# A graph network's count stage reordered: edge loads split by 96, 28 and one row, four count batches ahead of the products, half of the first weight sums on VectorE

## The reference

```python
# layer 0 (t5 norm, then RGCN with F = 286 columns and 2 relations)
out = x @ W_root + bias
for r in range(2):
    w = (edge_type == r)
    msg = h_src @ W_rel[r] * w[:, None]
    sums = segment_sum(msg, dst); cnt = segment_sum(w, dst)
    out = out + sums / maximum(cnt, 1.0)[:, None]
y = elu(out) @ wo_weight; h = x + y
# then x = layernorm(x + h)
# layer 1: the same with 8 relations of 1024 x 1024, a root product,
#          and a gate: z = [u, x] @ w_gate + b_gate; h = tanh(u) * z + x * (1 - z)
# then x = layernorm(x + h)
```

## Time and profile before

| | |
|---|---|
| median of 3 runs | 890.87 us (890.82 to 891.12) |
| the profiled execution | 891.17 us, of it the span 889.2 us |
| TensorE matmuls busy | 834.6 us (94%) |
| VectorE | 674.5 us (76%) |
| ScalarE | 447.7 us (50%) |
| POOL | 16.1 us (2%) |
| DMA moved | 63.42 MB, mean 71 GB/s |
| mean granted TensorE clock | 0.975 |

### The profile page before, as it was taken

One profiled execution on the slowest core, in us unless ns is written; L12 is line 12 of the kernel. 1 busy time (PEld: TensorE's weight loads), 2 busy tenths in 40 slices (PEclk: granted clock), 3 DMA queues, 4 the chain that ended last, 5 costly groups with the idle time before them and its releaser, 6 DMA issues.

```text
span 889.2 us, 16319 instructions
## 1 busy us (share of the span) xinstructions
PE 834.6 (94%) x6332; PEld 591.8 (67%) x6332; DVE 674.5 (76%) x975; ACT 447.7 (50%) x633; POOL 16.1 (2%) x38
## 2 busy tenths in 40 slices
PE   2569999899989999999999999999999999999996
PEld 1435574445876876876866867867868768769442
DVE  5985569689987778778778777677777787777877
ACT  3984555556465544445355356255354444445721
POOL 1000000000000000000000000000000000000000
PEclk9669999999999999999999999999999999999998
DMA  8100026120222021021120220220220210311302
GB/s 266 62 23 31 0 99 235 72 95 1 95 96 95 2 96 68 28 95 33 61 94 1 93 94 0 94 94 0 94 94 0 94 66 30 119 34 63 119 24 92
DMA packets 30734, 63.42 MB, mean 71 GB/s; under 512 B 1389, under 2 KB 5097, under 8 KB 30697
## 3 DMA queue, kind: packets, MB, share of 16 engines
q1 hardware_dynamic: 30181, 62.64, 19.9%
q10 hardware_dynamic: 516, 0.26, 0.1%
HBM read 57.71 MB, written 5.18 MB: 71 GB/s over the span
## 4 chain that ended last, share of the span: by engine, by line
PE 76%; DVE 16%; ACT 4%; issue 3%; DVEq 0%; POOL 0%; ACTq 0%; POOLq 0%
PE psP L1081 44%; PE psA L1151 19%; PE psP L928 5%; PE psA L917 3%; DVE wsplit L1326 2%; DVE wsplit L1320 2%; PE psP L1006 1%; DVE p_mem L1364 1%; PE psP L885 1%; DVE wsplit L1455 1%; PE psA L873 1%; DVE xT L1292 1%; DVE stats L1530 1%; DVE cu_mem L1574 1%; DVE p_mem L1363 1%
## 5 line engine op out<-in xcount | busy, mean ns | idle before, releaser
L1081 PE MATMUL psP<-wsplit,xT 128*128 128x256 f16 x2592 | 296.4, 273 | 3.2 <-ACT vec L767 2.8
L1081 PEld LDWEIGHTS psP<-wsplit,xT 128*128 128x128 f16 x2592 | 254.3, 98 | 37.5 <-issue 3.1
L1151 PE MATMUL psA<-p_mem,cu_mem 128*128 128x512 f16 x800 | 175.3, 379 | 0.0
L1081 PE MATMUL psP<-wsplit,x 128*128 128x256 f16 x1296 | 150.3, 273 | 1.7 <-DVE key_mem L1640 1.5
L1151 PEld LDWEIGHTS psA<-p_mem,cu_mem 128*128 (+1 forms) x800 | 78.2, 98 | 91.0
L1081 PEld LDWEIGHTS psP<-wsplit,x 128*128 128x128 f16 x1296 | 126.7, 98 | 16.8 <-issue 2.2
L1326 DVE SCALAR_TENSOR_TENSOR wsplit<-stage,sc,wsplit 128x1024 f16<-128x1024 f32 x90 | 114.8, 1279 | 27.2 <-ACT wsplit L611 27.2
L611 ACT ACTIVATE wsplit<-stage,sc 128x1024 f16<-128x1024 f32 x90 | 100.6, 1137 | 15.0 <-DVE sc L1228 9.1
L1605 DVE SCALAR_TENSOR_TENSOR cu_mem<-psA,coef,cu_mem 128x512 f32<-128x512 f32 x80 | 60.0, 750 | 32.9 <-PE psA L1151 30.9
L611 ACT ACTIVATE wsplit<-x,sc 128x1024 f16<-128x1024 f32 x54 | 61.7, 1143 | 39.2 <-PE psP L1081 32.5
L1326 DVE SCALAR_TENSOR_TENSOR wsplit<-x,sc,wsplit 128x1024 f16<-128x1024 f32 x54 | 69.2, 1282 | 10.3 <-ACT wsplit L611 10.2
(11 more groups left out here) (189 smaller groups left out, 800.8 us busy)
## 6 DMA issues: line engine op xcount, KB each, us to landing
stage<-in_L_gnn_weight SPq DMA_DIRECT2D x16, 2048.0 KB, 7.8
stage<-in_L_gnn_w_gate SPq DMA_DIRECT2D x4, 2048.0 KB, 7.8
x_home<-x SPq DMA_DIRECT2D x5, 512.0 KB, 2.6
x<-x_home SPq DMA_DIRECT2D x5, 512.0 KB, 5.6
stage<-in_L_gnn_W_rel SPq DMA_DIRECT2D x4, 572.0 KB, 11.1
x<-in_x SPq DMA_DIRECT2D x4, 512.0 KB, 9.6
xT<-in_L_gnn_root SPq DMA_DIRECT2D x1, 2048.0 KB, 8.0
stage<-in_L_gnn_root SPq DMA_DIRECT2D x1, 2048.0 KB, 7.8
```

Of the source, the lines that this page charges most:

```text
L1081: last = nc.tensor.matmul(psP[:, bank, (col + tt) * FB:(col + tt + 1) * FB], lhs[tt](a, c), split_block(n, b)[:, c, :], start=(first and t ...
L1151: last = nc.tensor.matmul(psA[:, (NT * h + t) % 2, :], cnt8[:, r, s, t * P:(t + 1) * P], p_part[h][a][:, s, :], start=(s == 0 and a == 0), ...
```

## The change

Three things are done together.

- `load_edges` takes three loads for each array: rows 0 to 95 with all 256 columns, rows 96 to 123 with all 256, and the last row's 160. There are twelve loads instead of eight, six on SP's queue and six on ACT's.
- `AHEAD` becomes 4. Tile 0 has three batches *behind* each of its four quarter products; tiles 1 to 4 have one batch ahead of each, as before.
- VectorE sums chunks 4 to 7 of the first weights with one reduction and two small steps; ScalarE sums 0 to 3.

With these, orders change. ScalarE squares four tiles before it spreads keys, spreads the two-type keys of all windows at once, and the eight-type keys of windows 40 to 319 after its sums. VectorE spreads the low bits of windows 40 to 319 after its sums. Table 6 stands between the low parts of chunks 3 and 4. The norm weights are transposed ahead of the x tiles, into a bank of `psP`. The order check's matmul stands after tile 0, the register loads ahead of the last tile.

```diff
-AHEAD = NB - 4 * NT
-FIRST = AHEAD + 2
+FIRST_PART = 3
+AHEAD = NB - 4 * (NT - 1) - 4 * FIRST_PART
...
+            def span(v, p0, p1):
+                return bass.AP(v.tensor, v.offset + p0 * RUN, [[RUN, p1 - p0], [1, SPAN]])
             for a, v in arrays:
-                engine.dma_start(edges[:, a, 0:RUN], v.rearrange("(p e) -> p e", e=RUN)).then_inc(loaded, 16)
+                engine.dma_start(edges[0:ROWS16, a, :], span(v, 0, ROWS16)).then_inc(loaded, 16)
             engine.wait_ge(edges_padded, 2)
             for a, v in arrays:
-                engine.dma_start(edges[0:EP - 1, a, RUN:SPAN],
-                                 v[RUN:EDGES].rearrange("(p e) -> p e", e=RUN)[:, 0:SPAN - RUN]).then_inc(loaded, 16)
+                engine.dma_start(edges[ROWS16:EP - 1, a, :], span(v, ROWS16, EP - 1)).then_inc(loaded, 16)
+                engine.dma_start(edges[EP - 1:EP, a, 0:RUN], v[EDGES - RUN:EDGES].unsqueeze(0)).then_inc(loaded, 16)
...
@@ ScalarE
-            square_x(0)
-            square_x(1)
-            spread_keys(0, EARLY)
-            square_x(2)
+            for t in range(4):
+                square_x(t)
+            spread_keys_8(0, EARLY)
+            spread_keys_2(0, NWIN)
             split_hi(0, 0, xT, X_GAIN)
-            spread_keys(EARLY, NWIN)
-            square_x(3)
+            square_x(4)
             split_hi(0, 1, xT, X_GAIN)
...
-            copy_batches(3, 4)
-            w0_sum(0)
-            copy_batches(4, 8)
-            w0_sum(1)
-            copy_batches(8, 10)
+            w0_sums_first()
+            copy_batches(3, AHEAD)
+            spread_keys_8(EARLY, NWIN)
             act.wait_ge(w0_scaled, 1)
             w0_high(0)
-            copy_batches(10, AHEAD)
             w0_high(1)
@@ TensorE
+            count_batches(3, AHEAD)
+            count_tile(0, count_first=False)
             pe.wait_ge(wrong_ready, 2)
+            pe.wait_ge(low_spread, 2)
             nc.tensor.matmul(psC[0:1, 0:RUN + KT], ones[0:EP, :], wrong, start=True, stop=True).then_inc(wrong_counted, 1)
-            count_batches(3, AHEAD)
+            with pe.Fori(1, NT - 1) as t:
+                count_tile(t)
             pe.wait_ge(flag_ready, 1)
             wrong_order = pe.value_load(flag[0:1, 0:1], min_val=0, max_val=EP)
-            count_tile(0)
-            with pe.Fori(1, NT) as t:
-                count_tile(t)
+            count_tile(NT - 1)
@@ VectorE
+            def w0_sums_second():
+                half = slice(DC // 2, DC)
+                dve.wait_ge(w0_loaded[1], 48)
+                step(nc.vector.tensor_reduce(am0[:, half], st0[:, half, :], AX.X, ALU.add, apply_absolute_value=True))
+                step(tt(am0[:, half], am0[:, half], lnwT[:, half], ALU.mult))
+                stt(am0[:, half], am0[:, half], -1.0, am0[:, half], ALU.mult, ALU.max).then_inc(w0_sums, 1)
...
             split_x_lo(4)
-            onehot_batches(5, 6)
...
+            dve.wait_ge(lnwT_ready, 1)
+            w0_sums_second()
+            spread_low(EARLY, NWIN, 2)
...
-            onehot_batches(AHEAD, FIRST - 1)
+            dve.wait_ge(keys8_spread, 2)
+            onehot_batches(AHEAD, AHEAD + 2)
...
             w0_low(0)
-            onehot_batches(FIRST - 1, FIRST)
+            onehot_batches(AHEAD + 2, AHEAD + 3)
             w0_low(1)
+            onehot_batches(AHEAD + 3, AHEAD + 2 * FIRST_PART)
...
             onehot_tile(0, first=True)
-            with dve.Fori(1, NT) as t:
+            onehot_batch(AHEAD + 4 * FIRST_PART, 0)
+            first_sums(0, 1)
+            dve.wait_ge(wrong_counted, 1)
+            nc.vector.tensor_reduce(flag[:, :], psC[0:1, 0:RUN + KT], AX.X, ALU.max).then_inc(flag_ready, 1)
+            for n in range(1, 4):
+                onehot_batch(AHEAD + 4 * FIRST_PART + n, n % 2)
+                if n == 2:
+                    first_sums(1, 0)
+            with dve.Fori(2, NT) as t:
                 onehot_tile(t)
```

More of the change, by code:

```diff
@@ L385, in scale_col, with block_batches @@
             return i if i <= U_WO else 2 + slot
-        def block_batch(t, n):
-            return 4 * t + (AHEAD + n)
+        def block_batches(t, n):
+            if isinstance(t, int) and t == 0:
+                return [(k, k % 2) for k in range(AHEAD + FIRST_PART * n, AHEAD + FIRST_PART * (n + 1))]
+            return [(4 * t + (NB - 4 * NT + n), n % 2)]
         def by_twos(engine, k0, k1, batch):
@@ L543, in square_x, with spread_keys_8, spread_keys_2 @@
                                      scale=1.0 / D).then_inc(rms_std_ready, 1)
-            def spread_keys(j0, j1):
+            def spread_keys_8(j0, j1):
+                act.wait_ge(keys_gathered, 1)
+                nc.scalar.activation(key_spread[:, j0:j1, 0:R1], psP[:, 4, j0:j1].unsqueeze(2).broadcast_to([P, j1 - j0, R1]),
+                                     ACT.Copy).then_inc(keys8_spread, 1)
+            def spread_keys_2(j0, j1):
                 act.wait_ge(keys_gathered, 2)
[L548 to L551, removed]
+                nc.scalar.activation(key_spread[:, j0:j1, R1:REL_ALL],
+                                     psP[:, 3, j0:j1].unsqueeze(2).broadcast_to([P, j1 - j0, R0]),
+                                     ACT.Copy).then_inc(keys2_spread, 1)
             def split_hi(k, t, dst, gain):
@@ L639, in _, with w0_sums_first @@
             st0, hi0, _ = unit_weights(U_W0)
-            def w0_sum(a):
+            def w0_sums_first():
                 act.wait_ge(lnwT_ready, 1)
[L644 to L648, removed]
+                act.wait_ge(w0_loaded[0], 48)
+                for c in range(DC // 2):
+                    nc.scalar.activation(w0_land[:, c, :], st0[:, c, :], ACT.Abs, scale=lnwT[:, c:c + 1],
                                          accum_out=am0[:, c:c + 1]).then_inc(w0_sums, 1)
@@ L692, in _ @@
             wo_sum()
+            act.wait_ge(flag_ready, 1)
+            wrong_order = act.value_load(flag[0:1, 0:1], min_val=0, max_val=EP)
             copy_tile(NT - 1)
@@ L934, in blocks_ready, with count_tile @@
                 pe.wait_ge(wlo_ready, n)
-            def count_tile(t):
+            def count_tile(t, count_first=True):
                 for n in range(4):
                     h, a = n // 2, n % 2
-                    count_batch(block_batch(t, n), n % 2)
+                    if count_first:
+                        for k, b in block_batches(t, n):
+                            count_batch(k, b)
                     if a == 0:
@@ L948, in count_tile @@
                         last.then_inc(q_full, 1)
+                    if not count_first:
+                        for k, b in block_batches(t, n):
+                            count_batch(k, b)
+            pe.wait_ge(lnw_loaded, 16)
+            nc.tensor.transpose(psP[:, 2, 0:DC], lnw[:, :], ident[0:DC, 0:DC]).then_inc(lnw_turned, 1)
             turn(0, 0, xs, xs_ready)
@@ L953, in _ @@
             turn(0, 2, xs, xs_ready)
+            pe.wait_ge(keys2_spread, 1)
+            pe.wait_ge(lnwT_ready, 1)
             count_batches(1, 2)
[L955 to L957 removed]
             turn(0, 3, xs, xs_ready)
@@ L1409, in _ @@
             spread_low(0, EARLY, 1)
+            dve.wait_ge(lnw_turned, 1)
+            nc.vector.tensor_copy(lnwT[:, :], psP[:, 2, 0:DC]).then_inc(lnwT_ready, 1)
             dve.wait_ge(consts_ready, 7)
-            dve.wait_ge(keys_spread, 2)
+            dve.wait_ge(keys8_spread, 1)
+            dve.wait_ge(keys2_spread, 1)
             onehot_batches(0, 1)
@@ L1464, in onehot_tile @@
                     if not (first and n < 2):
-                        onehot_batch(block_batch(t, n), n % 2)
+                        for k, b in block_batches(t, n):
+                            onehot_batch(k, b)
                     if n == 0 and not first:
```

33 lines of the change are left out of this document (13 added, 20 removed).

## The result

The changed kernel takes **892.91 us** (median of 17 runs, 891.76 to 894.47); the kernel before, run beside it, 891.47 us (17 runs, 890.64 to 892.92). The ratio is 1.0017, 95% interval 1.0009 to 1.0024: slower by 1.4 us. Forecast were 895.6 us, a change of +4.7. The sign is right, and the time lies in the range of 8 in 10, 890.0 to 898.5.

The account below looks back on a forecast made before the run. TensorE was taken as the bound from the second quarter product (62.66 us), VectorE close behind. Terms -9.4 + 4.6 + 9.5 = +4.7 on the median 890.87 gave 895.6 us; own range 893.5 to 897.2, 8 in 10 890.0 to 898.5.

Parts of the forecast that it names:

- the new wait: VectorE ahead of table 6, held by the count of batch 4 queued behind Q0: 4.5 us, 47.9 to 52.4.
- Edge loads: Kernel start: loads cut into 96, 28 and 1 rows bring the first table to 17.25 instead of 19.35.
- the rest of the span moves as a block: Behind the loop over tiles: nothing changes but a register load, so the rest shifts with the loop.
- What is queued there: VectorE and TensorE around Q0: table 6 waits 4.5 us; the second quarter product starts at 57.9, before 62.66.
- third rival: VectorE isn't held at table 6; Q4 at 67.8, total 888.1 us, 886.4 with POOL early; chance 0.09.
- Q4: Fifth of TensorE's 20 quarter products, numbered from 0; forecast to start at 75.35 against 70.59.
- Q0: First of TensorE's 20 quarter products; forecast to start at 47.9 instead of 57.29, 9.4 us sooner.
- Q1 at the low level: Second quarter product, run at TensorE's low clock after idling about 3.6 us: ends at 61.6, against 60.2 at high.
- The walk through tile 0: Quarter products with three batches behind each, tables waiting for counts: 17.45 us to Q4 instead of 7.93, +9.5.
- the register load: TensorE's load of the flag's register, now ahead of the last tile: taken at 0, covered by queued matmuls.
- Q5: Sixth of TensorE's 20 quarter products, the forecast's landmark: start at 78.4 against 73.67, +4.7 us.
- second rival: Smaller loss: POOL ready by 9.0 (-1.65), second quarter product at high clock (-1.9): +1.15, 892.0 us; chance 0.14.

Follow-up runs that it names:

- both ways of taking it away: Changed kernel with all eight low parts ahead of table 6: 886.66 us; or with TensorE counting batches 4 and 5 ahead of Q0: 885.60 us.
- the two counts moved forward: Changed kernel with TensorE counting batches 4 and 5 ahead of Q0 instead of behind it: 885.60 us, 0.9942 against the kernel before.
- the clock held up ahead of Q0: Changed kernel with 28 unread matmuls of 429 columns on TensorE until Q0: 891.48 us, 1.0014 against the kernel before.
- the delayed kernel: Kernel before with 20 unread matmuls on TensorE ahead of the degree matmuls: 894.58 us, 1.0036.
- the sums back on ScalarE: Changed kernel with all eight sums on ScalarE and no reduction on VectorE: 896.51 us, 1.0059 against the kernel before.

## Why the prediction was right and wrong

**The step that failed.** The new wait was there as forecast; terms of the sum were mis-sized. Forecast were +4.7 us, measured +1.4, so 3.3 are missing. The largest error is in step "Edge loads", which took 2.1 us off the start because it held POOL's identity at 10.62: by themselves these loads took 4.2 us off the kernel, and the identity was ready at 9.53 there and by 9.0 in the changed kernel. That is 2.1 of the 3.3. The rest of the change was put at 6.8 (4.7 + 2.1) and cost 5.6 us, 1.2 less. By the profiles it moved the degrees by 6.65 us (mean 119.63 against 112.98 with the edge loads alone), so up to there it was priced nearly right. What is missing lies mostly behind them, in a term that was put at nothing, "the rest of the span moves as a block": the rest was 1.0 us shorter than before in the mean of three profiles, by falls of the clock. Why they were fewer stays open. The single steps follow.

**Right: the new wait.** Step "What is queued there" said 4.5 us ahead of table 6; the three profiles of after have 4.65, 5.01 and 5.33. Its cause is shown, not argued: both ways of taking it away return far more than the 1.4 us lost (-5.9 and -7.0, of which -5.2 and -6.3 stand at the start of the degrees). The gap was named as the deciding place of the third rival too. With the two counts moved forward that rival's condition is met, and Q4 starts at 67.51 against its 67.8. The agreement is partly luck: Q0 is 1.5 us sooner than was assumed there (46.35 against 47.9), and the tables of tile 0 still wait for counts (0.25 and 0.71 us ahead of two of them), which its sum left out, and Q4 is slow (3.96).

**Right: Q1 at the low level, and tile 0.** From Q0 to Q1 were 10.1 us against 10.0 forecast (10.5 and 10.8 in the other two profiles). Q1 took 4.04. The prediction prices this level at 1.4 us in one place (61.6 against 60.2) and at 1.9 in another; the rows give 1.7 (4.04 against 2.36). From Q1 to Q4 were 17.50 against 17.45 (17.42 and 17.88). The walk through tile 0 holds with its gaps of VectorE's tables (0.86 and 0.62 at its end). The Trainium skill's TensorE: Matmul & The Clock Gate, section HAM oscillation, says that idle gaps between bursts of matmuls bring the clock down; the traces agree, in Q1 (after 3.47 us idle), and with the clock held up ahead of Q0, where Q1 falls back though Q0 ran at the high level.

**Right: the register load.** There is no gap on TensorE ahead of the last tile, and the way from Q5 to the degrees is 41.54 to 41.55 us in the profiles after and 41.78 to 41.80 in those before.

**Mis-sized: the start.** Step "Edge loads" put the first table 2.1 us sooner; it came 3.75 sooner in the mean. The landing was right (5.24, in the 5 to 6). What was taken too late was POOL's identity: I held it ready at 10.62, and it was ready at 8.76, 8.71 and 8.97. The gather therefore started at 8.82, 8.77 and 9.02, at the lower bound of 9.0. POOL's 9.35 us were "issue" in the profile, waiting for nothing visible, and I read them as a fixed cost; they shrank to 7.41 with the new loads. The second rival named this, and half of it happened: its other half, Q1 at the high level, did not. That its 892.0 lies so near to the result is partly luck. In the prediction's sum the start is worth 1.65 us, of which 0.64 is the point set for before: its first table comes at 19.99 in the mean of three, not at 19.35.

The Trainium skill's DMA: Bandwidth & Descriptors, section Rules for kernel authors, advises against two transfers to disjoint partition halves, since both halves run over all 16 engines. For this row count the measurement differs: the DMA share from 3 to 4 us is 0.57 instead of 0.34, and the loads alone gained 4.2 us. Its section on why a DMA increments its semaphore by 16 gives, by its rule, 5 engines for 125 rows and 16 for 96; the share of 0.34 before (5.4 of 16 engines) fits.

**Mis-sized: the reference point.** I took 73.67 for Q5 from one profile, the earliest of three (73.67, 74.38, 75.28). Against the mean of 74.44, the change at Q5 is +3.64; between the two first profiles it is +4.2. Had I set 78.4 against 74.4, +4.0 would have stood there. This is not a further error beside the start: both come from the one profile. I could not know this from one trace, but an uncertainty of 1 us on the starting point should have been in the text.

**Failed: "the rest of the span moves as a block".** As to work it does, by the delayed kernel. As to the clock it doesn't: the rest behind the start of the degrees was 1.0 us shorter in the mean of three, and 3.2 in the two first profiles, where before had two falls behind the loop and after none. In the second and third profiles each kernel has one. The counts of falls are 2, 1, 1 and 0, 1, 1. Whether the change itself makes the fall rarer, by shifting where the work stands when the gap comes, or whether that is chance, these six profiles can't tell. The mean granted clock, on record for every run, says that such differences are common: of 80 executions of before, 27 lie at 0.975 or 0.976, as the profile with two falls does, and 52 at 0.978 or 0.979, as those with one do; the 27 are 0.8 us longer in the median. It doesn't say where a fall lies. Of the variants, the edge loads alone, the sums back on ScalarE and the delayed kernel show one fall, the other five none. **This stays open.**

**Left out: time outside the span.** It is 2.0 to 2.1 us in the runs before and 1.8 in those after: -0.3 in the mean, and 1.8 with the edge loads alone as well.

In the prediction's own terms, by the means of three profiles: to Q0 -11.3 (forecast -9.4), from Q0 to Q1 +5.1 (+4.6), from Q1 to Q5 +9.9 (+9.5), together +3.64 (+4.7). Then -0.24 to the degrees, -1.04 behind them and -0.3 outside, all put at nothing: +2.1. The medians of all runs say +1.4; the difference is within what three profiles of a kind can place, given landmarks that wander by 1 to 2 us.

And by parts, from runs: edge loads -4.2; the reduction on VectorE +0.2 in the old order, within the intervals; the new order the rest, +5.4. More than that comes back when two counts move ahead of Q0 (7.0). The kernel that results (885.60) is 5.2 us below before; over the edge loads alone (0.9942 against 0.9953, intervals that overlap) its order gains nothing that these runs can tell.

## What to carry to other kernels

When a product is moved forward past small work, look at which buffers that small work releases and who is queued for them; here the way out cost nothing, since the counts fitted into idle time of the same engine. Look at the DMA share of a first load before taking its time as given: here a load of 125 rows was worth cutting into 96, 28 and 1, with all its columns in one load (4.2 us); other row counts weren't tried. For effects near 1 us on a long kernel, take several profiles of each side: one profile's landmark, and the number of clock falls in it, are off by as much.

## What the runs showed of the hardware

- POOL's first instruction behind its fills came 1.6 to 2.4 us sooner in the changed kernel, though its program ahead of it was the same: after an idle time of 9.35, 9.78 and 9.36 us before, and of 7.41, 7.49 and 7.74 after. With the edge loads alone it was 8.09, and 10.55 in the delayed kernel, which has the old loads. What it does in that time isn't shown.
- Behind the same gap of 1.83 us, or of 2.8 us, on TensorE the granted clock falls in some executions and not in others, at 1.5 to 1.7 us each time.
- Q4 of the first profile after ran slow (3.94 us) behind gaps of only 0.86 and 0.62 us; in the second and third it did not (Q5 2.8 us after Q4 instead of 4.2). With the two counts ahead of Q0 it ran slow too (3.96).
